# Cross-attention's row maxima: one bank for each slot in place of two banks for every second slot

## The reference

```python
q = (x @ Wq).reshape(B, N, HEADS, hd).transpose(0, 2, 1, 3)
k = (context @ Wk).reshape(B, M, HEADS, hd).transpose(0, 2, 1, 3)
v = (context @ Wv).reshape(B, M, HEADS, hd).transpose(0, 2, 1, 3)
scores = jnp.einsum('bhid,bhjd->bhij', q, k) * scale
scores = jnp.where(context_mask[:, None, None, :], scores, max_neg)
attn = jax.nn.softmax(scores, axis=-1)
out = jnp.einsum('bhij,bhjd->bhid', attn, v)
return out.transpose(0, 2, 1, 3).reshape(B, N, DIM) @ Wo
```

## Time and profile before

| | |
|---|---|
| median of 3 runs | 3476.01 us |
| profiled execution | 3473.2 us, span 3471.5 us |
| mean granted clock of TensorE | 0.972 of full speed |
| PE busy over the span | 3188.9 us (92%) |
| DVE | 2588.6 us (75%) |
| ACT | 2249.9 us (65%) |
| POOL | 1095.1 us (32%) |
| maxima of cross-attention | first at 1564.5 us, last at 2354.2 us |

### The profile page before, as it was taken

The page is one execution under the profiler, slowest core; times in us unless marked ns, Lnnn a source line. Parts: engine busy times, 40 slices in busy tenths (PEclk is TensorE's granted clock), DMA queues, the critical chain, the costliest instruction groups (busy, mean ns, idle before and its releaser), DMA issues.

```text
span 3471.5 us, 47183 instructions
## 1 busy us (share of the span) xinstructions
PE 3188.9 (92%) x15056; PEld 2499.6 (72%) x15056; DVE 2588.6 (75%) x4071; ACT 2249.9 (65%) x4127; POOL 1095.1 (32%) x1192
## 2 busy tenths in 40 slices
PE   5999999999999999979999999988989999942998
PEld 4878888888888888856666666655768888732887
DVE  5987878787877787757787878877864469888564
ACT  4876767676776767645777777765432256668665
POOL 1233242333333333344565555556500000000000
PEclk9999999999999999989999999999999999975999
DMA  3443444334434443346565665655712268889764
GB/s 122 167 158 121 129 149 125 128 119 155 122 126 133 134 136 125 95 134 119 117 114 106 125 120 115 124 102 171 233 74 111 113 224 298 327 342 407 267 239 177
DMA packets 273029, 555.49 MB, mean 160 GB/s; under 512 B 28025, under 2 KB 105857, under 8 KB 259473
## 3 DMA queue, kind: packets, MB, share of 16 engines
q1 hardware_dynamic: 268560, 544.08, 52.4%
q10 hardware_dynamic: 4224, 8.39, 0.6%
HBM read 322.72 MB, written 162.30 MB: 140 GB/s over the span
## 4 chain that ended last, share of the span: by engine, by line
PE 33%; DVE 9%; DMA 6%; issue 3%; ACT 2%; SPq 1%; POOL 1%; DVEq 0%; POOLq 0%; ACTq 0%
PE gu_acc L2637 7%; PE ca_mx L2551 3%; DMA gu_g<-gate 3%; DVE ca_negm L2127 3%; PE md_acc L2724 3%; PE md_acc L2725 3%; PE ca_pj L2533 3%; PE md_acc L2726 3%; PE ca_ov L2581 2%; PE ca_ov L2582 2%; PE ca_st L2569 2%; PE ca_pj L2522 2%; DVE ca_el L2142 1%; PE ca_ms L2541 1%; DMA gu_w_raw<-in_L_ffn_w_up_dram 1%
## 5 line engine op out<-in xcount | busy, mean ns | idle before, releaser
L915 POOL TENSOR_SCALAR sa_ex<-sa_ex,sa_rs 128x512 f32<-128x512 f32 x512 | 354.9, 693 | 907.8 <-DVE sa_rs L741 907.8
L736 DVE TENSOR_REDUCE sa_nm<-sa_st 128x1 f32<-128x512 f32 x512 | 350.2, 684 | 224.1 <-PE sa_st L1057 220.1
L578 ACT ACTIVATE sa_eh<-sa_tr 128x512 fp32r<-128x512 f32 x512 | 306.2, 598 | 295.1 <-PE sa_tr L1067 293.3
L1008 PE MATMUL sa_pj<-sa_xh,sa_w 128*128 128x512 f32 x1536 | 455.9, 416 | 3.0 <-DVE sa_xl L714 1.5
L2127 DVE TENSOR_REDUCE ca_negm<-ca_mx 128x2 fp32r<-128x1024 f32 x256 | 312.5, 1221 | 99.7 <-PE ca_mx L2551 95.9
L745 DVE TENSOR_TENSOR sa_el<-sa_tr,sa_eh 128x512 fp32r<-128x512 f32 x512 | 351.2, 686 | 40.9 <-ACT sa_eh L578 34.1
L571 ACT ACTIVATE sa_ex<-sa_st,sa_nm 128x512 f32<-128x512 f32 x512 | 350.9, 685 | 43.3 <-DVE sa_nm L736 39.4
L2420 POOL TENSOR_TENSOR ca_el<-ca_ex,ca_eh 128x512 fp32r<-128x512 f32 x256 | 349.2, 1366 | 62.6 <-ACT ca_eh L1916 62.2
L1908 ACT ACTIVATE ca_ex<-ca_st 128x512 f32<-128x512 f32 x512 | 296.1, 585 | 41.4 <-PE ca_st L2569 39.7
L1067 PE MATMUL sa_tr<-top_ident,sa_ex 128*128 128x128 f32 x2048 | 306.9, 272 | 1.8 <-POOL sa_ex L915 1.8
L1067 PEld LDWEIGHTS sa_tr<-top_ident,sa_ex 128*128 128x128 f32 x2048 | 254.3, 140 | 71.0 <-POOL sa_ex L915 4.3
(11 more groups left out here) (309 smaller groups left out, 7566.4 us busy)
## 6 DMA issues: line engine op xcount, KB each, us to landing
sa_w<-w_split SPq DMA_DIRECT2D x56, 1536.0 KB, 7.5
gate<-gu_ev SPq DMA_DIRECT2D x24, 1024.0 KB, 4.4
gu_g<-gate SPq DMA_DIRECT2D x48, 512.0 KB, 6.4
gate<-gu_g SPq DMA_DIRECT2D x48, 512.0 KB, 3.8
up<-gu_ev SPq DMA_DIRECT2D x24, 1024.0 KB, 5.7
md_ab<-gate SPq DMA_DIRECT2D x96, 256.0 KB, 6.5
md_ab<-up SPq DMA_DIRECT2D x96, 256.0 KB, 7.0
md_ab<-gate SPq DMA_DIRECT2D x44, 512.0 KB, 11.9
```

The lines of the kernel that those rows point to most:

```text
L578: nc.scalar.activation(eh[:, v % ER], tr[:, v % 2], ACT.Copy).then_inc(act_eh, 1)
L736: nc.vector.tensor_reduce(nm[:, u % U:u % U + 1], st[:, u % 2], AX_X, ALU.max, negate=True).then_inc(dve_mx, 1)
L915: nc.gpsimd.tensor_scalar(ex[:, u % U], ex[:, u % U], rs[:, u % U:u % U + 1], 1.0, ALU.mult, ALU.mult).then_inc(pool_n, 1)
L1008: yield nc.tensor.matmul(pj[:, bank], w[:, n % 2, m, part, k], xx[b % 2][:, k], start=(i == 0 and k == 0), stop=(i == 2 and k == DK - 1))
```

## The change

Each slot now has one score tile for the maxima and one reduction. PE computes tile m in its slot and waits that the reduction of tile m - 2, which used the same bank, is done. DVE reduces one bank in every slot, as the slot's first instruction, and waits for that one tile. The sums of the semaphores stay the same at the end of each section, so that what waits for all 16 maxima is unchanged.

```diff
             def maxima(m):
                 n, h, qt = m // U, m % U // NT, m % NT
-                e.wait_ge(pe_mx, m + 2)
-                nc.vector.tensor_reduce(negm[:, n % 2, qt:qt + 2, h], mx[:, :], AX_X, ALU.max,
-                                        negate=True).then_inc(dve_mx, 2)
+                e.wait_ge(pe_mx, m + 1)
+                nc.vector.tensor_reduce(negm[:, n % 2, qt, h:h + 1], mx[:, m % 2], AX_X, ALU.max,
+                                        negate=True).then_inc(dve_mx, 1)
...
-                if 0 <= m < U * N and m % 2 == 0:
+                if 0 <= m < U * N:
                     maxima(m)
...
-                if m >= 2 and m % 2 == 0:
-                    e.wait_ge(dve_mx, m)
+                if m >= 2:
+                    e.wait_ge(dve_mx, m - 1)
...
-                if 0 <= G + U - LM < U * N and (G - LM) % 2 == 0:
+                if 0 <= G + U - LM < U * N:
                     max_scores(G + U - LM)
-                    max_scores(G + U - LM + 1)
```

## The result

The changed kernel has a median of 3455.9 us over 4 runs (3454.0 to 3461.03), the kernel before, on the same chip, 3474.36 us over 4 (3472.17 to 3478.5). The ratio is 0.9945, with a 95% interval of 0.9932 to 0.9958: 18.5 us faster, where 24 (3452 us) were forecast. The profiled execution after took 3456.6 us, its span 3454.8 us, 16.7 us less than before.

The account below looks back on a forecast made before the run. PE was taken as the bound, so only its waits could be won: 21.7 + 5 + 1.5 + 0.5 = 28.7 us, less 4.7, kept as 24, from 3476.0 to 3452 us; own range 3436 to 3466, 8 in 10 within 3431 to 3479.

Parts of the forecast that it names:

- price of 0.16 us more for each wait: PE's stalls: each is 0.16 us longer than its gap, making 45 waits of 27.8 us into 35.0 us.
- Part 1: DVE: 512 one-bank maxima for 256 two-bank ones cost 0.09 us more a pair, 23 us, mostly hidden by idle time.
- The 11 pairs a batch: Where DVE never waits, about 24 of 100 us: the extra work of about 11 pairs is on the path, 1.0 us.
- Part 2: PE: 256 more matmuls wait for a semaphore; where it is satisfied they cost nothing.
- Part 3: Banks freed earlier: context section 1.6, lightest 0.5, two value sections 1.0 us saved; 3.1 a batch, 21.7 for seven.
- the waits that stand next: PE's waits for POOL's low parts and eviction of `ov`, 11.9 us in seven batches, will grow; 4.7 us taken off.
- Part 4: Start-up: PE and DVE overlap with one wait a bank, saving 5 of 5.6 us, plus 1.5 us for the clock.
- R1: Gaps closed at the maxima open at POOL and ACT; only value sections and start-up gain: 3474 us, chance 0.16.
- R2: Low parts reach POOL's locked port too early: 3497 us, chance 0.08; decides once their mean rises some 20 ns.
- sign of being wrong: For DVE's low parts: the forecast is wrong if L2142's mean rises from 936 ns.
- R3: All waits for the maxima gone and part of the port's lock waits too: 56 us saved, 3420 us, chance 0.11.
- R4: DVE's fixed price decides, all 256 pairs on the path: plus 23 less 12 us, 3487 us, chance 0.07.

Follow-up runs that it names:

- run 9: Changed kernel with one more tensor_reduce over 32 columns of the bank ahead of every second maximum: 3462.47 us, ratio 0.9957 to the kernel before.
- run 6: Changed kernel loading only half the bytes of the query input from the second batch on (work left out): 3449.31 us, ratio 0.9921 to the kernel before.
- runs 6 and 7: Half the query input's bytes loaded from the second batch on: in the changed kernel 3449.31 us (0.9921), in the kernel before 3475.13 us (0.9999).
- run 1: Kernel before with DVE's maxima split into two one-bank ones back to back, a wait for each bank, PE's pairs left: 3469.15 us, ratio 0.9977.
- run 8: Changed kernel with a one-column Vector memset of an unused tile behind every second maximum: 3463.09 us, ratio 0.9959 to the kernel before.
- run 5: The changed kernel once more, as it is, on the chip of runs 6, 8 and 10: 3460.39 us, ratio 0.9953 to the kernel before.

## Why the prediction was right, and where it was not

**The bound and the mechanism: right.** PE was the bound and its waits for the maxima were what the change could win. They fell by 22.3 us, further than the forecast's 27.8 to about 10. What remains is short (0.4 us at most), in odd slots as well.

**The number: nearer than its terms.** At the prediction's own price of 0.16 us more for each wait, the waits for the maxima went from 35.0 to 8.7 us in seven batches: 26.3 us won, where 21.7 were counted. The other waits grew by 11.1 us (eviction +13.8, DMAs +9.9, POOL's low parts -8.4, DVE's -4.2), where 4.7 were taken off. One term was 4.6 us too small and the other 6.4 too small, and they partly cancel: that is luck. The difference, 15.2 us, stands against 13.5 measured; these rows do not tell the rest.

**Part 1, the price: right in size, and mostly hidden.** The time between starts gives 0.07 to 0.09 us a pair, and little or none of it shows on the path (run 9). The 11 pairs a batch that it puts where DVE never rests are 9 by the trace: five start in the first of the two stretches and four in the second. The Trainium skill's rule ("VectorE: DVE Perf Modes", section "The TRN2 errata"), an estimate of 32 us, agrees with the busy time of L2127, which rose by 32.4 us; that time overlaps with the next instruction's start. The miss in the last two sections, +1.8 us in place of -0.5, is not shown to be this price: it goes with the clock, as said above.

**Part 2, waits on PE: right** as far as the rows go. Where the wait is satisfied, neighbours still start 0.23 to 0.24 us apart.

**Part 3.** The value sections went as forecast, 0.5 us each (24.83 to 24.34), but for three of fourteen, of 25.1 to 25.2 us: one begins at the lower clock behind the first DMA wait, and in two PE waits 0.6 and 0.7 us for the row of maxima (`ca_mrow`). The lightest gave 0.7, not 0.5. The context section is where the sum failed: forecast -1.6 us, measured -0.7, and +2.0 in the first batch. The working through DVE's rows held: the low parts start ahead of POOL and take 0.68 us, and with the load halved the section is 1.9 us shorter (run 6). Its total is loose, though: the terms written out, 0.5 and 1.0 us sooner less two times 0.25, do not add up to 1.6. What failed is the step behind it, the 4.7 us that I took off for "the waits that stand next". I looked for them among PE's waits of before, where only engines stand. The eviction grew by 11.2 us, while POOL's 7.1 and DVE's 2.3 went, 1.8 on balance. The largest newcomer, 8.6 us of two DMA waits, had no row before, because from 1600 us on the copy of the low queries always landed ahead of its use, in the context sections by 0.04 to 2.2 us. Its whole price, with the pieces' extra and what is queued behind, is 11 us (runs 6 and 7).

**Part 4, the start-up: right, then partly given back.** The waits for maxima fell from 4.5 to 1.4 us and the clock rose; 3.9 us were won of the 6.5, and 2.0 went again at the first DMA wait, with the lower clock behind it.

**The rivals.** R1, gaps that open at once at ACT: half right, in that the eviction took up 11 us, yet not to the whole of the gain. R2, the locked port: the low parts' mean did rise, 936 to 988 ns, by more than the 20 ns that were to decide it, and the kernel is faster all the same:

```profile
L2127 DVE TENSOR_REDUCE ca_negm<-ca_mx 128x1 fp32r<-128x512 f32 x456 | 307.3, 681 | 58.7 <-PE ca_mx L2551 56.6
L2142 DVE TENSOR_TENSOR ca_el<-ca_ex,ca_eh 128x512 fp32r<-128x512 f32 x229 | 226.3, 988 | 0.0
```

By sections, each low part counted once by its start and over the six later batches, the mean fell from 1026 to 824 ns in those with context. It rose in the value sections (from 886 and 889 to 965 and 958) and most in the lightest (from 982 to 1196). There the waiting at the port took DVE's idle time: DVE was busy in 81% of the lightest sections before and in 92% after, and they are 0.7 us shorter all the same. As a sign of being wrong the mean over all sections was badly chosen. R3 was out of reach: even with the load halved the waits for the eviction and the maxima add up to 21.7 us. R4 fell with run 9.

What stays open: whether the waits for the eviction (16 us) can be had at all, since covering them moved them to the maxima; and why run 1 wins 8 us by the finer release alone, of which I did not follow the rows slot by slot. Outside the context sections the copy of the low queries now lands as little as 0.2 to 0.3 us ahead of its use (four sections), so a further gain of that size would meet it there too.

## What to carry to other kernels

Where two engines hand a buffer to and fro, try to release and refill it in smaller pieces, and change the order on both sides together: the finer pieces with both orders kept won 8 us of 18, and with DVE's order alone changed 17 were lost. Before a stall is counted as won, look up how much margin every transfer has that is used behind it, issue to use against issue to landing; the waits in the profile list only those that are already late. A mean over sections with different bounds decides nothing: read it in the section where its engine never rests.

## What the runs showed of the hardware

A memset of one column (59 ns) ran beside a low part on DVE, and the next start stayed where it was, 0.61 us behind the low part's (run 8). A reduction of 32 columns of PSUM, shown as 184 ns, put its successor back by 0.10 to 0.11 us (run 9). A reduction of one bank is shown as 0.68 us and holds DVE for 0.60 to 0.61, one of two banks as 1.22 and 1.13 to 1.14. The copy of 256 KB landed 9.8 to 11.0 us behind its issue with no large load in front, 10.9 to 12.4 with one of 1024 KB issued 5.7 us ahead (in the batch shown), and 8.2 to 10.8 with that load halved. In the changed kernel's trace a stall of 1.88 us was followed by matmuls of 0.62 us in place of 0.40, at the lower of the clock's two levels, while stalls of 1.41 and 1.47 us later in it were not; nor was one of 3.03 us in run 5.
